# Rework of the seam between a graph layer and the first attention block: casts, transposes and bias work put in another order

## What is computed

```python
# first graph layer (two rounds)
h = A_norm @ h
h = h @ W_gcn[l] + b_gcn[l]
h = leaky_relu(h @ W_mlp[l] + b_mlp[l])
x = x + h
# second: h = relu(layernorm(x)), then four blocks of
y = cond_layer_norm(h, cond, s1_w, s1_b, b1_w, b1_b)      # xn * (1 + cond@sw+sb) + cond@bw+bb
q, k, v = y@wq+bq, y@wk+bk, y@wv+bv
h = h + (softmax over the edges of q.k) @ v @ wo + bo
...                                                        # then a two-layer MLP with the same conditioning
```

## Time and profile before

| | us |
|---|---|
| median of 3 runs | 868.13 (865.55 to 871.05) |
| profiled execution, its own time | 865.51 |
| its span, first to last instruction | 864.0 |
| PE busy in the span | 830.5 (96%) |
| DVE / ACT / POOL busy | 562.7 / 397.5 / 232.5 |

### The profile page before, as it was taken

The page is one execution under the profiler, slowest core; times in us unless marked ns, Lnnn a source line. Parts: engine busy times, 40 slices in busy tenths (PEclk is TensorE's granted clock), DMA queues, the critical chain, the costliest instruction groups (busy, mean ns, idle before and its releaser), DMA issues. The chain is left out here.

```text
span 864.0 us, 13175 instructions
## 1 busy us (share of the span) xinstructions
PE 830.5 (96%) x4222; PEld 631.3 (73%) x4223; DVE 562.7 (65%) x1228; ACT 397.5 (46%) x646; POOL 232.5 (27%) x258
## 2 busy tenths in 40 slices
PE   6999889999799999999999999999999999999998
PEld 3666546767578778777697777787786976688786
DVE  7999998649958666576667575774776666720210
ACT  4999984234446512355433365233663235531200
POOL 4000033208432224402236022334013424422200
PEclk9999999999899999999999999999999999999999
DMA  8989966534224735533727329255348388020101
GB/s 186 211 212 239 263 156 165 145 98 114 97 68 93 205 89 160 145 105 112 181 87 178 96 52 233 74 156 141 99 147 194 106 218 219 13 98 1 49 13 37
DMA packets 59350, 113.44 MB, mean 131 GB/s; under 512 B 4372, under 2 KB 4936, under 8 KB 59292
## 3 DMA queue, kind: packets, MB, share of 16 engines
q1 hardware_dynamic: 42108, 79.00, 38.4%
q10 hardware_dynamic: 17184, 33.69, 11.9%
HBM read 105.33 MB, written 7.34 MB: 130 GB/s over the span
## 5 line engine op out<-in xcount | busy, mean ns | idle before, releaser
L683 POOL TENSOR_TENSOR wl<-wraw,wh 128x512 fp32r<-128x512 f32 x140 | 181.1, 1327 | 358.9 <-ACT wh L757 346.4
L688 POOL TENSOR_TENSOR rstd<-ve,half 128x1 f32<-128x1 f32 x48 | 26.3, 550 | 211.2 <-DVE ve L1146 210.9
L1803 PE MATMUL ring<-ohs,ohd 128*128 128x512 f32 x312 | 78.0, 401 | 2.8 <-DVE ohs L1317 2.8
L1803 PEld LDWEIGHTS ring<-ohs,ohd 128*128 128x128 f32 x312 | 57.8, 190 | 27.4 <-issue 14.8
L1295 DVE SCALAR_TENSOR_TENSOR ohd<-iota,dstT,vals 128x256 fp32r x156 | 69.5, 483 | 2.9 <-issue 1.8
L757 ACT ACTIVATE wh<-wraw 128x2048 fp32r<-128x2048 f32 x35 | 66.8, 1910 | 8.1 <-DMA wraw<-in_L_gnn_root 4.5
L782 ACT ACTIVATE yT_h<-ring 128x512 fp32r<-128x512 f32 x32 | 19.0, 598 | 97.9 <-PE ring L1719 97.9
L806 ACT ACTIVATE ohs<-iota,minus_srcT 128x512 fp32r<-128x512 f32 x78 | 52.2, 713 | 9.0 <-issue 6.4
L1730 PE MATMUL mix_ps<-quad,att_shift 120*32 120x512 f32 x384 | 50.1, 603 | 0.0
L1701 PE MATMUL ring<-yT_h,wh 128*128 128x512 f32 x128 | 49.8, 389 | 0.0
L1701 PE MATMUL ring<-yT_l,wh 128*128 128x512 f32 x128 | 49.8, 389 | 0.0
(11 more groups left out here) (384 smaller groups left out, 2149.6 us busy)
## 6 DMA issues: line engine op xcount, KB each, us to landing
quad<-in_L_gnn_basis SPq DMA_DIRECT2D x60, 960.0 KB, 9.9
wraw<-in_L_gnn_m_w ACTq DMA_DIRECT2D x8, 1024.0 KB, 10.0
mix_scratch<-mixed SPq DMA_DIRECT2D x128, 32.0 KB
wraw<-in_L_gnn_wv ACTq DMA_DIRECT2D x4, 1024.0 KB, 5.1
wraw<-in_L_gnn_wq ACTq DMA_DIRECT2D x4, 1024.0 KB, 5.3
wraw<-in_L_gnn_wk ACTq DMA_DIRECT2D x4, 1024.0 KB, 5.3
wraw<-in_L_gnn_wo ACTq DMA_DIRECT2D x4, 1024.0 KB, 5.4
wraw<-mix_scratch ACTq DMA_DIRECT2D x4, 1024.0 KB, 5.7
```

What stands on the lines that cost most here:

```text
L683: last = g.tensor_tensor(wl[s][:, k, :], wraw[s][:, k, :], wh[s][:, k, :].bitcast(F32), ALU.subtract)
L1803: last = te.matmul(ring[:, banks[b], :], ohd[:, s, b, :], ohs[:, s, :], start=False, stop=False)
```

## The change

It touches the seam and block 0 only.

- **ACT.** The cast of weight 3 moves from behind the G tiles to behind the Y tiles, that of weight 4 (`wv`) from ahead of the adjacency rows to ahead of the G tiles. The cast of `wq` moves out of block 0 and stands between `leak(1, 0)` and `leak(1, 1)`. The load of `wk` is issued behind `leak(1, 3)`. `block_input(2)` and `(3)`, and in block 0 the order of turned rows and values, follow the new order of PE. `take_set` of the mixing moves from head 2 to behind turn 2.
- **POOL.** `low_weight(4)` moves ahead of the adjacency work. The low part of `wq` is made in three pieces (`low_part`) between the inverse roots.
- **DVE.** The four mask updates go behind value 2 and the high part of q0; `step_weights` goes to the end of the attention. `conditioned` 0 stands ahead of `first_layer_out(3)`, and turn, value, statistics and conditioning alternate.
- **PE.** Condition a0 is made ahead of H(1,3). Turn 0, condition a1 and one mixing group follow, then value 0's twelve matmuls (`value_rows`), then turn 1, then value 0's bias (`value_bias`). Values 1 and 2 are interleaved with turns 2 and 3 in the same way. Of the four mixing groups (6,2), (6,3), (7,0) and (7,1), (6,3) goes behind condition a2, and (7,0), which stood ahead of head 3's transposes, behind value 2.
- **SP.** The load of `quad` group (7,0) is issued as soon as its buffer is free (after group (6,1)), ahead of the store of x; before it stood behind the condition and bias loads of block 1.

```diff
-    o = [("Ta", 1)] + ln("a", 2) + ln("a", 3) + [("v", 0), ("v", 1), ("Ta", 2), ("Ta", 3), ("v", 2)]
+    if first:
+        o = [("Ta", 1), ("v", 0)] + ln("a", 2) + [("Ta", 2), ("v", 1)] + ln("a", 3) + [("Ta", 3), ("v", 2)]
...
             def block_loads(i, nxt, last):
                 t = i * BLOCK_SETS + EARLY_SETS
                 if i:
                     load_group(t, 2)
+                else:
+                    load_group(t + 1, 0)
+                    sp.wait_ge(tile_taken, n0.base + n0.at[("H", 1, NT - 1)] + 1)
+                    sp.dma_start(rows(x_s), x[:]).then_inc(x_stored, 16)
...
-            low_weight(W1, slot(W1))
...
+            root_and_mean(ENTRY_X[0], 0)
+            root_and_mean(ENTRY_X[1], 1)
+            inverse_root(ENTRY_XL[0], 0)
+            root_and_mean(ENTRY_X[2], 2)
+            inverse_root(ENTRY_XL[1], 1)
+            root_and_mean(ENTRY_X[3], 3)
+            low_part(W1 + 1, slot(W1 + 1), (0,))
+            inverse_root(ENTRY_XL[2], 2)
+            low_part(W1 + 1, slot(W1 + 1), (1,))
+            inverse_root(ENTRY_XL[3], 3)
+            low_part(W1 + 1, slot(W1 + 1), (2, 3))
...
             leak(1, 0)
+            hw(W1 + 1)
             leak(1, 1)
             block_input(0)
             leak(1, 2)
             block_input(1)
             leak(1, 3)
+            lw(W1 + 2)
+            high(n0, n0.base, ("Ta", 0), yT_h[:, :, 0:P])
+            block_input(2)
...
-            for j in range(NT):
+
+            def edge_mask(j):
                 dve.wait_ge(cnt_act, j + 1)
                 v.scalar_tensor_tensor(mask[:, j, :], ln_c[:, j, :], 1.0 / SCALE, mask[:, j, :], ALU.mult, ALU.add)
...
             first_layer_out(2)
+            dve.wait_ge(ct_stored, 32)
+            conditioned(n0, n0.base, "a", 0, ENTRY_XL[0])
+            first_layer_out(3)
+            low(n0, n0.base, ("Ta", 0), HI_AHEAD, yT_l[:, :, 0:P], yT_h[:, :, 0:P])
             first_layer_stats(2)
...
+                if first:
+                    transposed("a", 1)
+                    value(0)
+                    block_input_stats(2)
+                    conditioned(T, b, "a", 2, i * 8 + 10)
+                    block_input_stats(3)
+                    transposed("a", 2)
+                    value(1)
+                    conditioned(T, b, "a", 3, i * 8 + 11)
+                    transposed("a", 3)
+                    value(2)
+                    edge_mask(0)
+                    edge_mask(1)
...
+            for t in range(NT):
+                if t == NT - 1:
+                    pe.wait_ge(emb_step, 9)
+                    condition(n0, B, "a", 0, 1)
+                tile0(("H", 1, t), [bias_to_rows(3, bias_rows)] + products(hb_h[1], hb_l[1], t, wh[s], wl[s]))
+            transpose_rows(n0, B, "a", 0)
+            condition(n0, B, "a", 1, 1)
+            mix_group(EARLY_SETS, 2)
...
+                if i == 0:
+                    taken(n0, n0.base, ("Ta", 0))
+                    value_rows(0, w)
+                    taken(n0, n0.base, ("Ba", 1))
+                    first_rows()
+                    value_bias(0)
+                    condition(T, b, "a", 2, 1)
+                    mix_in_block(1)
+                    value_rows(1, w)
+                    transpose_rows(T, b, "a", 2)
+                    value_bias(1)
+                    condition(T, b, "a", 3, 1)
+                    value_rows(2, w)
+                    transpose_rows(T, b, "a", 3)
+                    value_bias(2)
                     mix_in_block(1)
```

More of the change, by code:

```diff
@@ L83, in bank, with l1_order @@
         return self.banks[name] if self.banks else self.at[name] % RING
-def l1_order(last):
+def l1_order(last, first=False):
     ln = lambda s, t: [("S" + s, t), ("B" + s, t)]
@@ L1014, in block_highs @@
                     mean_value(h - 1)
-                    if h == 2:
+                    if h == 2 and not first:
                         take_set(t)
@@ L1040, in block_highs @@
                     norm_rows("a", 0)
-            block_input(2)
-            high(ahead, ahead.base, ("Ta", 0), yT_h[:, :, 0:P])
             block_highs(0, False, True)
@@ L1587, in attention_block @@
                 probs_T(HEADS - 1)
+                if first:
+                    step_weights()
                 mean_value(HEADS - 1)
@@ L1978, in columns_product, with value_rows, value_bias, value @@
                          three(cols(w[0], k, m), cols(w[1], k, m), rh[:, k, :], rl[:, k, :])])
-                def value(t, w):
+                def value_rows(t, w):
                     if t:
                         done(("Ta", t))
-                    out = begin(T, b, ("v", t))
-                    part(out, [p for k in range(KT) for p in three(cols(yT_h, k, t), cols(yT_l, k, t), w[0][:, k, :], w[1][:, k, :])],
+                    part(begin(T, b, ("v", t)),
+                         [p for k in range(KT) for p in three(cols(yT_h, k, t), cols(yT_l, k, t), w[0][:, k, :], w[1][:, k, :])],
                          first=True)
+                def value_bias(t):
                     if t == 0:
                         pe.wait_ge(brow_ready, i + 1)
-                    part(out, [bias_to_rows(0, brow)], last=True).then_inc(tile_ready, 1)
+                    part(bank_of(("v", t)), [bias_to_rows(0, brow)], last=True).then_inc(tile_ready, 1)
+                def value(t, w):
+                    value_rows(t, w)
+                    value_bias(t)
                 def query_key(h):
@@ L2117, in attention_block @@
                         transpose_rows(T, b, "a", 0)
[L2120 to L2125 removed]
+            attention_block(0, False, GROUPS - 1)
             for i in range(1, BLOCKS - 1):
```

169 lines of the change are left out of this document (85 added, 84 removed).

## The result

The kernel after is faster by 0.8%: a median of 861.83 us (6 runs, 859.19 to 863.80) beside 868.64 for the kernel before (6 runs), a ratio of 0.9917 with a 95% interval of 0.9892 to 0.9942, so a gain of 7.2 us, between 5.0 and 9.4. The prediction was 865.1, a gain of 3.0. The profiled execution after took 862.01 us, its span is 860.4.

The account below looks back on a forecast made before the run. PE loses 9.7 us between H(1,0) and the first query product, set by DVE's chain. That product 2.3 us earlier, plus 1.0 for the moved group, less 0.3, gives 3.0: 868.1 to 865.1 us, range 861.5 to 869.0.

Parts of the forecast that it names:

- rival 1: Seam: wq lands in time, by 212.1 say, so the gain is 5.0 to 5.6 us, 862.6 us; chance 0.25.
- the wq load's lateness: ACT's cast ahead of `leak(1, 1)`: sharing with the quad load makes wq land 3 us late, at 214.2.
- equal time: DMA engines: wq and quad loads get equal time, so wq lands 2.1 us late, at 213.3.
- equal bytes: DMA engines: both loads get equal bytes, wq lands 4.0 us late, at 215.2; 866.1 us, chance 0.12.
- Rival 4: ACT: the wq cast holds it much longer, decides from a landing at 217.2 on; up to 870.0 us, chance 0.08.
- DVE's work from the second out to q0: Seam, second `first_layer_out` to first query product: DVE's instructions 21.3 us plus waits and hops, 24.6 us, before 27.1.
- DVE's start: Seam's beginning: masks moved, DVE free by 210.4; second `first_layer_out` could begin at 214.1, but waits for ACT until 216.7.
- `step_weights` and the masks: DVE's load: masks of 3.6 us move behind value 2; `step_weights`, 3.0 us for its products, leaves the seam at no cost.
- POOL and wk: End of the seam: wk's low part is ready at 244.4, so PE waits 0.3 to 0.4 us.
- Rival 3: POOL too late with wk, all pieces at the slow rate: 2.2 us more than counted, 867.3 us; chance 0.07.
- rival 2: Seam: the granted clock falls again behind the wait ahead of turn 0; gain 1.1, 867.0 us; chance 0.13.
- The mixing group: PE: group (7,0) done in the seam saves 1.0 us at head 3 and fills waiting time in the seam.

Follow-up runs that it names:

- experiment 1: The kernel before once more, with no edit: 869.69 us, ratio 1.0016 to the kernel before.
- experiment 2: Kernel before with only DVE relieved (mask updates and `step_weights` at their new places): 864.38 us, ratio 0.9950 to the kernel before.
- experiment 3: Kernel after with ACT's cast of wq moved behind `leak(1, 2)`: 861.21 us, ratio 0.9913 to the kernel before.
- experiment 4: Kernel after with the wq load placed behind the adjacency rows in the code, which delayed nothing: 860.94 us, ratio 0.9908 to the kernel before.
- experiment 5: Kernel after with the four mask updates back ahead of the first `first_layer_out`: 861.35 us, ratio 0.9885 to the kernel before.
- experiment 6: Kernel after with `step_weights` back in the seam, between values 0 and 1: 861.48 us, ratio 0.9905 to the kernel before.
- experiment 7: Kernel after with the casts of weights 3 and 4 and wv's low part back at their old places: 862.11 us, ratio 0.9888 to the kernel before.
- experiment 9: Kernel after with the edits of experiments 5 and 7 together (masks and casts back): 865.73 us, ratio 0.9955 to the kernel before.
- experiment 10: Kernel after with masks, casts and `step_weights` all back, leaving the new order: 864.96 us, ratio 0.9958 to the kernel before.
- experiment 11: Kernel after with DVE's conditioned rows ahead of the value parts and the wq cast later: 861.60 us, ratio 0.9913 to the kernel before.
- Experiment 12: Kernel after with mixing group (6,1) one U tile earlier, so the quad load precedes the wq load: 865.10 us, ratio 0.9951 to the kernel before.
- experiment 8: Kernel after with the wq load held by a semaphore until H(1,0) is done: 868.52 us, ratio 0.9989 to the kernel before.

## Why the prediction was right or wrong

- **Side and size.** "Within 1%, and faster" came true, and 861.83 is just inside the range, at its lower end. But the gain was 3.0 in the forecast and about 7 in truth. What happened is rival 1, which I gave 0.25 and a time of 862.6.
- **The step that failed: the wq load's lateness.** I took 3 us, between the 2.1 of equal time and the 4.0 of equal bytes, with bounds of 0 and 7.9. Measured is 0.7 (6.1 us to landing, before 5.4; 1.0 to 1.1 against the 5.1 and 5.0 of experiments 1 and 2), which costs 0.3 us of the seam. In the profiled executions of experiments 3 to 7 and 9 to 11, where the quad load follows it too, the wq load landed in 5.4 to 6.0 us; without a quad load behind it, in experiments 1 and 2, in 5.1 and 5.0. I let the quad's bytes flow from 1.3 us behind its issue, and shared the engines' time by a rule of equal turns from there on. Measured, its queue moved nothing for 3 us, until the wq load had moved 0.87 of its 1.05 MB; the traces of experiments 3, 5, 6 and 11, asked the same way, show the same. The load that was first went through almost undisturbed, and the quad load landed in 9.6 us (8.9 to 9.3 in the others) instead of 7.4. Experiment 12 turned the order of the two round, and the lateness went with it. The rule of the Trainium skill, DMA: Bandwidth & Descriptors, section on queues, rings and completion order, that I had weighed, with its 4.0 us and 866.1, was further off than my middle; the trace shows no turns in 210 to 213 us, where only one of the two queues moved bytes. Whether SP's queue had packets ready by then no view shows, so why the second load's bytes hold back isn't settled.
- **The mechanism itself was right.** The cast stands in ACT's order ahead of the slope, and each us of lateness costs one: experiment 8 held it 4.9 us and lost 4.9, before the clock's part. Rival 4 put the point where the gain is used up at a landing at 217.2, 10.0 us behind H(1,0). In experiment 8 it landed 9.6 us behind H(1,0), and the kernel took 868.52, no change. (In part that is luck: the gains that I had left out were spent by the clock that I had left out too.)
- **DVE's work from the second out to q0**: 24.6 us predicted, 24.2 measured, and 24.06 to 24.32 in all kernels with the new order whose clock did not fall. This sum from rows was good to 2%.
- **DVE's start**: free well ahead of the first slope, as predicted. The second out at 7.16 us behind H(1,0) is in rival 1's 6.9 to 7.4, not at the forecast's 9.5. This term alone is 2.3 of the 3.8 us by which the gain was forecast too small (3.0 against the 6.8 between the two medians).
- **`step_weights` and the masks**: I took what they cost before, 3.0 and 3.6 us, as their price. It was so for the order of before (experiment 2 wins 3.2 us of the seam). In the new order it is not: alone, either may go back for 0 to 0.2 us (experiments 5 and 6), because POOL is silent beside them. What the change really bought there is that DVE's work and POOL's low parts don't lie at the same time.
- **POOL and wk**: 0.3 us predicted, none measured; PE never waits for wk's low part. Rival 3 did not happen.
- **The clock** stays at 1.00, as I forecast against rival 2: the longest wait is 1.07 us where I had 3.7. Experiments 8 to 10, with 3.3 to 6.0 us of wait at turn 0, show it fall again each time, and q0 then 0.8 to 2.1 us further behind the second out (in 10 with `step_weights` in it), where I had counted 1.9 for rival 2. So this part came true by luck: had the wait been the 3.7 us that I forecast, the clock would by these three have fallen, and rival 2 would have been the case.
- **The mixing group**: +1.0 us at head 3 predicted. The first turned tile of the next norm begins 43.15 us behind q0, before 44.29 (44.07 in experiment 1): 0.9 to 1.1. Confirmed, nothing comes to wait in its place.
- **The sum by parts.** Seam 36.41 - 31.36 = 5.05. From q0 to the end of the span 618.6 us, before 620.4 and 620.2: 1.6 to 1.8, of which 0.9 to 1.1 is the group. The other 0.6 lies behind that turned tile, in pieces of 0.1 us or less from block to block: from it to the end are 576.1 us in both executions of before and 575.5 after (575.4 and 575.5 in experiments 5 and 6). What makes it stays open. 5.1 + 1.7 = 6.8, the distance of the medians. So of the 3.8 us that the forecast lacked, 2.3 are the load, 0.4 DVE's sum, 0.3 POOL, and 0.6 to 0.8 this rest with what the group gave beyond 1.0.
- **The baseline.** I subtracted the gain from the median, not from the profiled execution. That was right, and it hid a trap: the profiled execution of before was one of the few without the early fall of the clock.

## What to carry to other kernels

A duration in the trace belongs to an instruction and its neighbours: before you price a step that moves, look at what lies beside it now and what will then (an instruction of 0.22 us may stand there with 1.05). A cast that waits for a load holds all that stands behind it, so it should be put behind the urgent work, or its load issued far ahead; but here a second load issued 1 us later took little from the first (0.7 us where 3 were forecast). And when two spans differ, look at the granted clock in every stretch before you put the difference down to the change: here 3 to 4 us of it came and went at 139 to 144 us, some 65 us ahead of the seam and 20 ahead of the first instruction that the change moves (the cast of weight 3, at 164 us in the kernel after).

## What the runs showed of the hardware that I had not expected

- With two loads of 1024 KB (ACT's queue) and 960 KB (SP's) in flight, the wq load, which came first, took 5.4 to 6.1 us instead of 5.0 to 5.4, the quad load 8.9 to 9.6 instead of 7.4. With their order turned round it was 6.8 and 7.5. The later one's queue moved no bytes until the earlier one was nearly through.
- A DMA issued in ACT's order began 2.3 us before an activation that stands ahead of it (experiment 4).
- The same four mask updates took 2.49, 3.59 or 4.72 us, by how much of POOL's work lay beside them: before, three of the four took 0.68 us each and the last, beside POOL's pieces, 1.79. `ve`, a product on 128x1, took 0.15 us beside POOL, and the 128x4 products of `step_weights` 0.22 each alone against 1.05.
- A fall of the granted clock to 0.50 with PE shown busy ahead of it and all through it (139 to 141.5 us: 2.50 us busy of 2.50). It is there in twelve of the fourteen profiled executions, in some later and shorter (0.60 in 141.5 to 144 us in experiment 7), and missing in two, one of the kernel before and one of experiment 6. In the two executions with it shown above DVE did 0.33 us of work in 139 to 141.5, in the one without 1.29; which is cause and which effect no run here tells.
